# Loading and turning the weights of a two-layer kernel ahead of its first transposes, and handing out the first slots after two tiles

## The chip, the cores and the metric

One core of a Trainium2 chip runs the whole program. The metric is the device time of one execution in microseconds (us), the median of three runs. The engines are TensorE (PE), VectorE (DVE), ScalarE (ACT), GpSimd (POOL) and SyncE (SP, which here only issues DMAs). Waits between them are semaphore waits written into each engine's own list of instructions.

## The reference, cut to what matters

```python
xn = _layernorm(x)                        # x: 16 sequences of 256 tokens, 128 wide
s = _L0_attn_ref(xn, ...)                 # a complex linear recurrence over time
g = _silu(_L0_ffn_ref(xn, ...))           # 32 experts, top 4, plus a shared expert of width 256
x = x + s * g
xn = _layernorm(x)
s = _L1_attn_ref(xn, wq, bq, wk, bk, wv, bv)      # softmax attention
g = _silu(_L1_ffn_ref(xn, ...))           # 8 experts, top 2
x = x + s * g
```

In the first layer only the experts that a token chose are computed. So tokens must be routed: every token gets a row ("slot") in a list sorted by expert for each of its 4 choices.

## The kernel before, in words

The 4096 tokens are 32 tiles of 128. They are handled in two halves of 16 tiles (HT = 16, NH = 2), in groups of 4 tiles (GT = 4). For each half:

1. SP loads the rows of x (L403 to L405, all eight groups first, then the router's weights, then twelve loads of weights, L422, all counted on `w_in`). After them come two copies of `expert_sel`, six fills of `slot_rows0` with zeros (L434), the experts' weights and six fills of `slot_rows1`.
2. DVE normalises the rows (`norm0`, L1183 to L1206). PE transposes each group (`turn_half`, L608), ACT copies the result out of PSUM (`copy_half`, L956), PE multiplies it with the router's weights (L580), ACT copies the logits (L945).
3. DVE finds the four highest logits of each tile (`route`, L1224 to L1233), group by group, and writes `picked`, ones where an expert was chosen. PE counts (`ranks`, L593): bank 6 gets how many tokens of the same tile stand before each token, bank 7 the totals of each tile. From them DVE works out the slots: it copies bank 7 to SBUF turned to expert-major (L1239), makes a running sum over the tiles (L1240), the first tile of each expert (L1244 to L1250), adds that to all sums (L1251), adds bank 6 (L1253), and then picks out the four slots of every token in two pieces, first 4 tiles and then 12 (L1258 to L1270). Each piece raises `slots_ready`. After the first piece it also hands `tile_ex` to PE, which returns the expert of every slot tile.
4. POOL waits for the zero fills of the half (`filled`) and for `slots_ready`, and sends every tile's rows to their slots with indirect DMAs (L549), 4 for each tile, 64 for each half. Before tile 4 it waits for the second piece.

In the first half PE does the second layer's weights after the ranks (L620 to L635: a product of wq and wk, a transpose of wv, four columns with biases, eight transposes and some small products, into banks 2 to 5), and ACT copies them to SBUF after `exp_top` (L968 to L972). Then the shared expert of the first half runs (`shared_in`, `shared_out`, L648 to L661; ACT's silu L979, DVE's product L1309 and its gated result L1314), while POOL sends. In the second half, norm, transposes and logits follow, then the route of the second half with the shared expert's steps set between its links (`beside`), and three more recurrences (L1337 to L1345). Then 48 stages of expert work follow, 24 for each half (PE L718, L743, L726, L734; ACT L1000, L1006, L1024, L1015; DVE L1404), which read the slots that POOL wrote, and the gathers of their results (POOL L563), and at last the second layer.

SP starts loading the slots of a half when all 64 sends of that half have landed (`sent`).

The order of all this is written out by hand. Every engine runs its own list in order, and a wait holds all that is behind it on that engine.

Of the kernel before, what the change touches and what calls it, by code (L numbers as in the profile page):

```python
# [22 lines left out]
P = 128  # L23
# [22 lines left out]
EPS = 1e-5  # L46
SCALE = float(P) ** -0.5
# [79 lines left out]
def build(nc, x, phazor, phazor_init, last_re, last_im, router_w, w_gate, w_up, w_down, sh_gate, sh_up,  # L127
# [10 lines left out]
    with ctx:  # L138
# [69 lines left out]
        tot_em = route_tmp[:, 0, :].rearrange("p (e t) -> p e t", e=E0)  # L208
# [77 lines left out]
        zero_set = sem("zero_set")  # L286
        filled = [sem(f"filled{r}") for r in range(NH)]
# [109 lines left out]
        def _(sp):  # L397
# [4 lines left out]
            for g in range(NG):  # L402
                sp.dma_start(x_tok[:, g * GT:(g + 1) * GT, :],  # L403
                             x_rows[:, g * GT:(g + 1) * GT, :]).then_inc(x_in[g], 16)
# [19 lines left out]
            assert n == N_W  # L424

# [58 lines left out]
        def _(pool):  # L484
# [57 lines left out]
            for r in range(NH):  # L542
                pool.wait_ge(filled[r], 16 * N_FILL)
                for t in range(HT):
                    if t in (0, GT):
                        pool.wait_ge(slots_ready, r * 2 + 1 + t // GT)
# [22 lines left out]
        def _(pe):  # L569
# [14 lines left out]
            def ranks(r):  # L584
# [3 lines left out]
                for g in range(HT // GT):  # L588
                    pe.wait_ge(picked_ready, r * HT // GT + g + 1)
                    of = picked[:, g * GT * TOP0:(g + 1) * GT * TOP0, :].rearrange("p (t k) e -> p t k e", k=TOP0)  # L590
                    for to, rows_before in ((6, not_before), (7, ones_bf)):
                        for k in range(TOP0):
                            mm = pe.matmul(ps[:, to, g * w:(g + 1) * w], rows_before[:], of[:, :, k, :],  # L593
                                           start=(k == 0), stop=(k == TOP0 - 1))
# [19 lines left out]
            turn_half(0)  # L614
            ranks(0)

            pe.wait_ge(w_in, 16 * N_W)
            pe.wait_ge(lg_sb, NG // NH)

            pe.matmul(ps[:, 2, 0:P], raw1[:, 0, :], raw1[:, 1, :], start=True, stop=True)  # L620
            pe.transpose(ps[:, 2, P:2 * P], raw1[:, 2, :], ident[:])
            pe.matmul(ps[:, 2, 2 * P:2 * P + 1], raw1[:, 0, :], bqk[:, 1:2], start=True, stop=True)
            pe.matmul(ps[:, 2, 2 * P + 1:2 * P + 2], raw1[:, 1, :], bqk[:, 0:1], start=True,
                      stop=True).then_inc(wT_ps, 1)
            for j in range(CH1):
                last = pe.transpose(ps[:, 3, j * P:(j + 1) * P], raw_fc[:, j, :], ident[:])
# [11 lines left out]


            tile_ids(0)  # L640
            pe.wait_ge(wT_sb, 4)
# [288 lines left out]
        def _(sc):  # L930
# [34 lines left out]
            copy_half(0)  # L965
            exp_top(0)
            sc.wait_ge(wT_ps, 4)
            a.copy(w1T[:], bank(2, 2 * P + 2)).then_inc(wT_sb, 1)  # L968
            a.copy(fcT[:].rearrange("p a b -> p (a b)"), bank(3)).then_inc(wT_sb, 1)
            a.copy(prT[:].rearrange("p a b -> p (a b)"), bank(4)).then_inc(wT_sb, 1)  # L970
            a.copy(g1T[:], bank(5, E1))
            a.copy(bv_all, ps[0:3, 5, P:P + VW]).then_inc(wT_sb, 1)  # L972

# [200 lines left out]
        def _(dve):  # L1174
# [3 lines left out]
            v.memset(zeros[:, 0:GW], 0.0).then_inc(zero_set, 1)  # L1178

# [32 lines left out]
            def route(r, beside=None):  # L1212
# [7 lines left out]
                for g in range(HT // GT):  # L1220
# [8 lines left out]
                    if g == HT // GT - 1:  # L1229
# [9 lines left out]
                link(v.tensor_copy(tot_em, bank(7).rearrange("p (t e) -> p e t", t=HT)))  # L1239
                link(v.tensor_tensor_scan(cum_em.rearrange("p e t -> p (e t)"), not_first.rearrange("p e t -> p (e t)"),  # L1240
                                          tot_em.rearrange("p e t -> p (e t)"), 0.0, ALU.mult, ALU.add))
# [9 lines left out]
                link(v.tensor_tensor(cum_em, cum_em,  # L1251
                                     tiles_e[:].rearrange("p (e a) -> p e a", a=1).to_broadcast([P, E0, HT]), ALU.add))
                link(v.tensor_tensor(pos, bank(6).rearrange("p (t e) -> p t e", t=HT),  # L1253
                                     cum_em.rearrange("p e t -> p t e"), ALU.add))

                for c, (a, b) in enumerate(((0, GT), (GT, HT))):
# [39 lines left out]
            v.memset(ones_bf[:], 1.0)  # L1296
            v.memset(ones[:], 1.0)
            link(v.memset(not_first, 1.0))
            link(v.memset(not_first[:, :, 0:1], 0.0))
# [324 lines left out]
```

## Time and profile before

| what | us |
|---|---|
| median of three runs (711.32 to 712.45) | 712.23 |
| the profiled execution, whole | 712.29 |
| its span in the trace | 710.5 |
| busy: PE | 404.0 (57%) |
| busy: DVE | 324.1 (46%) |
| busy: POOL | 269.1 (38%) |
| busy: ACT | 259.3 (36%) |

No engine is busy all the time, so the shares alone name no bound. The page must be read by stage: its second part, 40 slices of 17.8 us with a digit for each engine's busy share, has POOL at 7 for slices 4 to 6 and 10 to 14 while the other engines fall to 0 in some of the same slices. What stands in those stretches has to be read in the timeline, engine by engine.

### The profile page before, as it was taken

How to read it: one execution, taken by the hardware profiler on the slowest of the kernel's cores; microseconds unless marked ns; L12 is line 12 of the kernel's file. 1: busy time of each engine (PE TensorE's matmuls, PEld its weight loads, DVE VectorE, ACT ScalarE, POOL GpSimd, SP SyncE). 2: the span in 40 equal slices, each digit the busy share in tenths (PEclk: the TensorE clock that was granted, in tenths of full speed). 3: DMA queues.
4: the chain of work that ended last, by engine and by line, in shares of the span. 5: the costliest groups of instructions: out<-in, count | busy, mean ns of one | idle time of the engine just before them, and what ended most of it. 6: DMA issues, size and time to landing. Idle time of an engine off the chain costs nothing. (4 is left out here: it accounts for less than half of the span.)

```text
span 710.5 us, 8856 instructions
## 1 busy us (share of the span) xinstructions
PE 404.0 (57%) x2582; PEld 364.4 (51%) x2582; DVE 324.1 (46%) x1167; ACT 259.3 (36%) x505; POOL 269.1 (38%) x324
## 2 busy tenths in 40 slices
PE   0873020676332019999512929299721674897996
PEld 0752020565321019999512919298610563786885
DVE  7871200486740015765000415068600491988853
ACT  1410000241000006767201515166411372886985
POOL 7467775001777730000474262500577166000000
PEclk9977555688655559999865968689955697998999
DMA  7999212000112114552521524242211011000000
GB/s 187 362 278 403 71 52 74 30 0 9 48 63 68 52 44 134 168 170 95 168 62 52 175 78 134 74 134 90 64 52 53 19 54 51 16 16 15 10 23 24
DMA packets 45903, 65.17 MB, mean 92 GB/s; under 512 B 8586, under 2 KB 23331, under 8 KB 45859
## 3 DMA queue, kind: packets, MB, share of 16 engines
q1 hardware_dynamic: 37666, 47.83, 21.1%
q0 software_dynamic: 8192, 16.79, 7.8%
q8 instruction: 23, 0.38, 0.2%
q14 instruction: 22, 0.17, 0.1%
HBM read 28.93 MB, written 35.65 MB: 91 GB/s over the span
## 5 line engine op out<-in xcount | busy, mean ns | idle before, releaser
L549 POOL DMA_INDIRECT slot_rows<-xn_tok,slot_of x128 | 125.6, 981 | 104.9 <-DVE slot_of L1270 66.4
L563 POOL DMA_INDIRECT onehot<-expert_rows,slot_of x64 | 61.8, 966 | 185.0 <-DMA expert_rows<-zeros 131.5
L1404 DVE TENSOR_TENSOR act<-sg,ps 128x384 f32<-128x384 f32 x48 | 26.6, 554 | 161.2 <-issue 101.0
L563 POOL DMA_INDIRECT route_tmp<-expert_rows,slot_of x64 | 60.7, 948 | 36.2 <-issue 19.0
L743 PE MATMUL ps<-w_gu,raw_fc 128*128 x192 | 41.0, 363 | 41.8 <-ACT raw_fc L1000 38.7
L734 PE MATMUL ps<-w_dn,actT 96*128 x384 | 54.0, 286 | 18.3 <-issue 15.9
L1006 ACT ACTIVATE sg<-ps 128x384 f32<-128x384 f32 x48 | 23.5, 491 | 106.8 <-remote 67.7
L661 PE MATMUL ps<-shd,hs_h 128*128 128x128 f32 x128 | 21.5, 321 | 70.1 <-issue 40.1
L734 PEld LDWEIGHTS ps<-w_dn,actT 96*128 96x128 f32 x384 | 49.2, 201 | 19.7 <-issue 19.6
L743 PE MATMUL ps<-w_gu,raw_pr 128*128 x192 | 40.2, 358 | 31.9 <-issue 31.7
L661 PEld LDWEIGHTS ps<-shd,hs_h 128*128 128x128 f32 x128 | 19.7, 228 | 73.8 <-issue 41.3
L743 PEld LDWEIGHTS ps<-w_gu,raw_fc 128*128 128x128 f32 x192 | 35.3, 214 | 43.1 <-issue 42.9
L979 ACT ACTIVATE hs_t<-ps 128x512 f32<-128x512 f32 x16 | 9.4, 597 | 118.3 <-remote 81.7
L743 PEld LDWEIGHTS ps<-w_gu,raw_pr 128*128 128x128 f32 x192 | 34.8, 211 | 32.9 <-issue 32.9
L1565 DVE TENSOR_TENSOR rows<-rows,ps 128x1024 f32<-128x1024 f32 x16 | 19.5, 1219 | 70.3 <-PE ps L886 45.0
L820 PE MATMUL ps<-prT,rows 128*128 128x128 f32 x256 | 36.4, 293 | 16.4 <-issue 10.8
L820 PEld LDWEIGHTS ps<-prT,rows 128*128 128x128 f32 x256 | 32.7, 203 | 19.5 <-issue 19.3
L726 PE MATMUL ps<-ident,act 128*96 128x128 f32 x192 | 31.1, 288 | 19.5 <-issue 19.5
L1015 ACT COPY zeros<-ps 128x512 f32<-128x512 f32 x48 | 28.1, 586 | 28.2 <-PE ps L734 16.0
L718 PE MATMUL ps<-ident,rows 128*128 128x128 f32 x192 | 33.1, 301 | 5.5 <-DMA rows<-slot_rows 3.9
L726 PEld LDWEIGHTS ps<-ident,act 128*96 128x96 f32 x192 | 23.0, 134 | 21.1 <-issue 20.5
L1024 ACT COPY actT<-ps 96x512 f32<-96x512 f32 x48 | 28.0, 584 | 11.3 <-remote 10.6
(242 smaller groups left out, 919.2 us busy)
## 6 DMA issues: line engine op xcount, KB each, us to landing
slot_rows<-zeros SPq DMA_DIRECT2D x12, 1024.0 KB, 9.7
rows<-slot_rows SPq DMA_DIRECT2D x48, 256.0 KB
expert_rows<-zeros SPq DMA_DIRECT2D x48, 256.0 KB, 2.0
x_tok<-in_L_attn_x_dram SPq DMA_DIRECT2D x8, 256.0 KB, 4.9
slot_rows<-xn_tok,slot_of POOLq DMA_INDIRECT x128
out_dram<-raw_fc SPq DMA_DIRECT2D x16, 128.0 KB
w_dn<-in_L_ffn_w_down_dram SPq DMA_DIRECT2D x1, 1536.0 KB
onehot<-expert_rows,slot_of POOLq DMA_INDIRECT x64
```

The costliest lines, as they stand in the source:

```text
L549: g.indirect_dma_start(out=slot_rows[r], out_offset=bass.IndirectOffsetOnAxis(ap=slot_of[:, n:n + 1], axis=0), in_=xn_tok[:, r * HT + t, : ...
L563: g.indirect_dma_start(out=gath[b % 4][:, j, :], out_offset=None, in_=expert_rows[r], in_offset=bass.IndirectOffsetOnAxis(ap=slot_of[:, n: ...
L661: mm = pe.matmul(ps[:, 4 + u, j * P:(j + 1) * P], hs_h[u][:, c, j * P:(j + 1) * P], shd[:, c, :], start=(c == 0), stop=(c == 1))
L718: mm = pe.transpose(ps[:, 0, j * P:(j + 1) * P], rows[slot][:, j * P:(j + 1) * P], ident[:])
L726: mm = pe.transpose(ps[0:I0, 5, j * P:(j + 1) * P], act[u][:, j, :], ident[:])
L734: mm = pe.matmul(ps[:, 6, j * P:(j + 1) * P], actT[u][:, j * P:(j + 1) * P], w_dn[:, bass.ds(e[j] * P, P)], start=True, stop=True)
L743: mm = pe.matmul(ps[:, 1 + 2 * u + j // 2, (j % 2) * 256:(j % 2) * 256 + 2 * I0], exT[u][:, j * P:(j + 1) * P], w_gu[:, bass.ds(e[j], 1), ...
L820: mm = pe.matmul(ps[:, 3, j * P:(j + 1) * P], hg[u][:, c, j * P:(j + 1) * P], prT[:, c, :], start=(c == 0), stop=(c == CH1 - 1))
L1006: a.activation(sg[u][:].rearrange("p (a b) i -> p a b i", a=2), ps[:, 1 + 2 * u:3 + 2 * u, :].rearrange("p a (b i) -> p a b i", b=2)[:, :, ...
L1015: a.copy(eo[slot], bank(6)).then_inc(e_out, 1)
L1024: a.copy(actT[u][:], ps[0:I0, 5, :]).then_inc(e_aTs, 1)
L1404: v.tensor_tensor(act[u][:].rearrange("p (a b) i -> p a b i", a=2), sg[u][:].rearrange("p (a b) i -> p a b i", a=2), ps[:, 1 + 2 * u:3 + 2 ...
```

## The change

- SP loads x's rows of the first half, then the router's weights, then the twelve loads of weights, and x's rows of the second half last.
- DVE clears `ones_bf`, `ones` and `not_first` at the start and not after `norm0(0)`.
- PE waits for all twelve loads and turns the weights before the first half's transposes, into banks 6, 7, 4 and 5. ACT copies them before it copies the first transposes. PE's ranks wait for those copies.
- PE writes the totals into bank 7 expert-major, so that DVE's copy L1239 goes and the running sum reads PSUM.
- The two pieces of slots are of 2 and 14 tiles (`FIRST = 2`), and the additions L1251 and L1253 are made for each piece. POOL waits for the second piece before tile 2.

```diff
+FIRST = 2
 ...
-            for g in range(NG):
-                sp.dma_start(x_tok[:, g * GT:(g + 1) * GT, :],
-                             x_rows[:, g * GT:(g + 1) * GT, :]).then_inc(x_in[g], 16)
+            def load_x(r):
+                for g in range(r * NG // NH, (r + 1) * NG // NH):
+                    sp.dma_start(x_tok[:, g * GT:(g + 1) * GT, :],
+                                 x_rows[:, g * GT:(g + 1) * GT, :]).then_inc(x_in[g], 16)
+
+            load_x(0)
             sp.dma_start(rw[:, 0:E0], router_w).then_inc(rw_in, 16)
...
             assert n == N_W
+            load_x(1)
...
-                    if t in (0, GT):
-                        pool.wait_ge(slots_ready, r * 2 + 1 + t // GT)
+                    if t in (0, FIRST):
+                        pool.wait_ge(slots_ready, r * 2 + 1 + t // FIRST)
...
-                            mm = pe.matmul(ps[:, to, g * w:(g + 1) * w], rows_before[:], of[:, :, k, :],
-                                           start=(k == 0), stop=(k == TOP0 - 1))
+                            if to == 6:
+                                into, chosen = ps[:, 6, g * w:(g + 1) * w], of[:, :, k, :]
+                            else:
+
+                                into = bank(7).rearrange("p (e t) -> p e t", t=HT)[:, :, g * GT:(g + 1) * GT]
+                                chosen = of[:, :, k, :].rearrange("p t e -> p e t")
+                            mm = pe.matmul(into, rows_before[:], chosen, start=(k == 0), stop=(k == TOP0 - 1))
...
-            turn_half(0)
-            ranks(0)
-
             pe.wait_ge(w_in, 16 * N_W)
-            pe.wait_ge(lg_sb, NG // NH)
+            pe.wait_ge(ones_set, 1)
+
+            pe.matmul(ps[:, 6, 0:P], raw1[:, 0, :], raw1[:, 1, :], start=True, stop=True)
...
+            turn_half(0)
+            pe.wait_ge(wT_sb, 4)
+            ranks(0)
 
             tile_ids(0)
-            pe.wait_ge(wT_sb, 4)
...
-            copy_half(0)
-            exp_top(0)
             sc.wait_ge(wT_ps, 4)
-            a.copy(w1T[:], bank(2, 2 * P + 2)).then_inc(wT_sb, 1)
+            a.copy(w1T[:], bank(6, 2 * P + 2)).then_inc(wT_sb, 1)
...
+            copy_half(0)
+            exp_top(0)
...
             v.memset(zeros[:, 0:GW], 0.0).then_inc(zero_set, 1)
+            v.memset(ones_bf[:], 1.0)
+            v.memset(ones[:], 1.0).then_inc(ones_set, 1)
+            link(v.memset(not_first, 1.0))
+            link(v.memset(not_first[:, :, 0:1], 0.0))
...
-                link(v.tensor_copy(tot_em, bank(7).rearrange("p (t e) -> p e t", t=HT)))
                 link(v.tensor_tensor_scan(cum_em.rearrange("p e t -> p (e t)"), not_first.rearrange("p e t -> p (e t)"),
-                                          tot_em.rearrange("p e t -> p (e t)"), 0.0, ALU.mult, ALU.add))
+                                          bank(7), 0.0, ALU.mult, ALU.add))
...
-                link(v.tensor_tensor(cum_em, cum_em,
-                                     tiles_e[:].rearrange("p (e a) -> p e a", a=1).to_broadcast([P, E0, HT]), ALU.add))
-                link(v.tensor_tensor(pos, bank(6).rearrange("p (t e) -> p t e", t=HT),
-                                     cum_em.rearrange("p e t -> p t e"), ALU.add))
-
-                for c, (a, b) in enumerate(((0, GT), (GT, HT))):
+                for c, (a, b) in enumerate(((0, FIRST), (FIRST, HT))):
+                    link(v.tensor_tensor(cum_em[:, :, a:b], cum_em[:, :, a:b], tiles_e[:]
+                                         .rearrange("p (e a) -> p e a", a=1).to_broadcast([P, E0, b - a]), ALU.add))
+                    link(v.tensor_tensor(pos[:, a:b, :], ps[:, 6, a * E0:b * E0].rearrange("p (t e) -> p t e", e=E0),
+                                         cum_em[:, :, a:b].rearrange("p e t -> p t e"), ALU.add))
```

## Rows read from the trace of the kernel before

**Rows 1.** The page's head.

```profile
span 710.5 us, 8856 instructions
```

**Rows 2.** Timeline, first half's sends: start, duration, instruction [idle before, releaser].

```profile
38.80 1.23 POOL L549 DMA_INDIRECT slot_rows<-xn_tok,slot_of  x1 [12.09 <-DVE slot_of L1270]
...
97.22 0.60 ACT L979 ACTIVATE hs_t<-ps 128x512 f32<-128x512 f32 x1 [33.73 <-remote]
...
119.33 0.97 POOL L549 DMA_INDIRECT slot_rows<-xn_tok,slot_of  x1 [0.31 <-issue]
...
128.75 1.08 ACT L979 ACTIVATE hs_t<-ps 128x512 f32<-128x512 f32 x2 [30.93 <-remote]
```

**Rows 3.** Timeline, the second half's sends.

```profile
174.66 0.97 POOL L549 DMA_INDIRECT slot_rows<-xn_tok,slot_of  x1 [54.36 <-DVE slot_of L1270]
...
204.93 0.37 ACT L982 COPY xnT<-ps 128x256 f32<-128x256 f32 x1 [3.26 <-PE ps L670]
...
214.78 0.58 ACT L1000 COPY raw_pr<-ps 128x512 f32<-128x512 f32 x1 [8.33 <-remote]
...
256.21 0.97 POOL L549 DMA_INDIRECT slot_rows<-xn_tok,slot_of  x1 [0.30 <-issue]
...
263.77 0.58 ACT L1000 COPY raw_fc<-ps 128x512 f32<-128x512 f32 x1 [6.51 <-remote]
```

**Rows 4.** Timeline, DVE, the first half's route from the ranks on.

```profile
30.01 0.69 DVE L1239 COPY route_tmp<-ps 128x512 f32<-128x512 f32 x1 [1.08 <-PE ps L593]
...
33.35 0.69 DVE L1251 TENSOR_TENSOR route_tmp<-route_tmp,tiles_e 128x512 f32<-128x512 f32 x1
34.08 1.00 DVE L1253 TENSOR_TENSOR route_tmp<-ps,route_tmp 128x512 f32<-128x512 f32 x1
35.11 0.90 DVE L1258 TENSOR_TENSOR onehot<-picked,route_tmp 128x128 f32<-128x128 bf16 x4
36.05 0.69 DVE L1262 TENSOR_REDUCE top_f<-onehot 128x16 f32<-128x512 f32 x1
...
37.68 0.17 DVE L1270 CUSTOM_DVE_ANT_0 slot_of<-slot_of,slot_a 128x32 uint16<-128x32 uint16 x1
...
40.98 1.75 DVE L1262 TENSOR_REDUCE top_f<-onehot 128x48 f32<-128x1536 f32 x1
...
43.92 0.21 DVE L1270 CUSTOM_DVE_ANT_0 slot_of<-slot_of,slot_a 128x96 uint16<-128x96 uint16 x1
```

**Rows 5.** Timeline, DVE, the ends of the two pieces in the second half.

```profile
173.71 0.17 DVE L1270 CUSTOM_DVE_ANT_0 slot_of<-slot_of,slot_a 128x32 uint16<-128x32 uint16 x1
...
187.78 0.21 DVE L1270 CUSTOM_DVE_ANT_0 slot_of<-slot_of,slot_a 128x96 uint16<-128x96 uint16 x1
```

**Rows 6.** Timeline, loads, first transposes and the weights; the transposes of the second half.

```profile
14.38 0.51 SPq L422 DMA_DIRECT2D raw_pr<-in_L_ffn_w_proj_dram  x1
...
16.00 2.04 PE L608 MATMUL ps<-ident,xn_tok 128*128 128x128 f32 x8 [16.00 <-DVE xn_tok L1206]
...
17.12 0.58 ACT L956 COPY xnT<-ps 128x512 f32<-128x512 f32 x1 [7.81 <-PE ps L608]
...
29.81 0.44 PE L620 MATMUL ps<-raw 128*128 128x128 f32 x2
...
32.25 0.37 ACT L968 COPY w1T<-ps 128x258 f32<-128x258 f32 x1 [2.54 <-PE ps L635]
...
33.53 0.25 ACT L972 COPY mth<-ps 3x129 f32<-3x129 f32 x1
...
141.48 0.63 PE L608 MATMUL ps<-ident,xn_tok 128*128 128x128 f32 x4
```

**Rows 7.** Timeline, DVE, first and last of the four groups' top-4 search.

```profile
20.12 0.47 DVE L1224 MAX8 top<-logits 128x8 f32<-128x32 f32 x4
...
28.25 0.69 DVE L1233 TENSOR_TENSOR picked<-iota_e,top_i 128x512 bf16<-128x512 f32 x1
```

**Rows 8.** Silus L1006 alone in one window: ACT busy (count), granted clock, DMA.

```profile
270.00:334.00 64.00, 9.80 (x20) 1.00 0.48 152
```

More of the change, by code:

```diff
@@ L207, in build @@
         route_tmp = sb("route_tmp", [P, 4, HT * E0])
-        tot_em = route_tmp[:, 0, :].rearrange("p (e t) -> p e t", e=E0)
         cum_em = route_tmp[:, 1, :].rearrange("p (e t) -> p e t", e=E0)
@@ L286, in build @@
         zero_set = sem("zero_set")
+        ones_set = sem("ones_set")
         filled = [sem(f"filled{r}") for r in range(NH)]
@@ L612, in turn_half @@
                 logits_of((r + 1) * NG // NH - 1)
-            turn_half(0)
-            ranks(0)
             pe.wait_ge(w_in, 16 * N_W)
-            pe.wait_ge(lg_sb, NG // NH)
[L620 to L623, printed above, removed]
+            pe.wait_ge(ones_set, 1)
+            pe.matmul(ps[:, 6, 0:P], raw1[:, 0, :], raw1[:, 1, :], start=True, stop=True)
+            pe.transpose(ps[:, 6, P:2 * P], raw1[:, 2, :], ident[:])
+            pe.matmul(ps[:, 6, 2 * P:2 * P + 1], raw1[:, 0, :], bqk[:, 1:2], start=True, stop=True)
+            pe.matmul(ps[:, 6, 2 * P + 1:2 * P + 2], raw1[:, 1, :], bqk[:, 0:1], start=True,
                       stop=True).then_inc(wT_ps, 1)
             for j in range(CH1):
-                last = pe.transpose(ps[:, 3, j * P:(j + 1) * P], raw_fc[:, j, :], ident[:])
+                last = pe.transpose(ps[:, 7, j * P:(j + 1) * P], raw_fc[:, j, :], ident[:])
             last.then_inc(wT_ps, 1)
@@ L963, in copy_half @@
                              ACT.Sigmoid).then_inc(sh_gated, 1)
-            copy_half(0)
-            exp_top(0)
             sc.wait_ge(wT_ps, 4)
-            a.copy(w1T[:], bank(2, 2 * P + 2)).then_inc(wT_sb, 1)
-            a.copy(fcT[:].rearrange("p a b -> p (a b)"), bank(3)).then_inc(wT_sb, 1)
+            a.copy(w1T[:], bank(6, 2 * P + 2)).then_inc(wT_sb, 1)
+            a.copy(fcT[:].rearrange("p a b -> p (a b)"), bank(7)).then_inc(wT_sb, 1)
             a.copy(prT[:].rearrange("p a b -> p (a b)"), bank(4)).then_inc(wT_sb, 1)
@@ L1295, in _ @@
             norm0(0)
[L1296 to L1299, printed above, removed]
             dve.wait_ge(pool_c, 7)
```

## The prediction

> **What bounds the kernel now.** I read the page's slices first, then the timeline of POOL, then that of ACT in the same stretches. The span is 710.5 us [rows 1]; the profiled execution took 712.29 us, 0.06 above the median of the runs, so a sum made against it stands for the median too. The reader is to see two bursts. POOL's 64 sends of the first half start at 38.80 and the last starts at 119.33 [rows 2], a step of 80.53 / 63 = 1.28 us each. Those of the second half run from 174.66 to 256.21 [rows 3]. Nothing in the trace makes a send shorter than this. The first send of each burst is released by DVE's slot numbers, L1270 [rows 2, 3]; neither the zero fills nor the ids came last. Inside the bursts ACT, and with it PE and DVE, comes to a near stop for a reason that the profile gives only as "remote": an idle of 33.73 us before one silu [rows 2], 8.33 us before one copy [rows 3], while the producer had long finished. They run again shortly after the burst: ACT takes up at 128.75, which is 8.4 us after the last send's end (119.33 + 0.97), and at 263.77, which is 6.6 us after 256.21 + 0.97 [rows 2, 3]. Between the bursts (128.75 to 174.66) the work is a chain through DVE and PE that ends in the second half's slots. So the end of the program is, to first order: start of burst one + burst one + the chain + burst two + a tail. An edit is worth what it does to the starts and lengths of the bursts.
>
> **Edits with one answer.** The early clears (four DVE instructions, under 1 us in all) go into the time in which DVE waits for its first data; at the old place they delayed nothing that was last, since the first logits came later. I cost them at nothing. If that cover were gone they would cost that 1 us. The second half's rows are loaded last, some 8 us later than before, but DVE reads them only after the first route ends at 44.13 [rows 4], so nothing waits. SP's list has the same number of loads ahead of the zero fills, so the fills start as before, and POOL's first wait had ended before 38.80.
>
> **Shorter chain to the first slots (in both halves).** Two slopes come from rows. L1262 takes 0.69 us for 512 elements and 1.75 for 1536 [rows 4], so 1.04 ns for an element and 0.16 fixed. L1258 takes 0.90 for four of 128 [rows 4], and I give it the same slope. Then:
> - L1239 goes: 0.69 us and a link's gap of 0.04, as between L1251 and L1253 [rows 4]: 0.73.
> - L1251 for 2 tiles, 64 elements, by that law 0.23 against 0.69: 0.46 less.
> - L1253 for 64 elements: between 1.00 / 8 and its full 1.00; its fixed part and its own slope give about 0.26, so 0.74 less.
> - L1258 at 64 elements: 4 x 64 x 1.04 ns = 0.27 less. L1262 at 256: 0.27 less.
> Sum 2.47 us less. Against it stands the scan, which now reads PSUM. No row has that. The nearest is L1253, 1.00 with a PSUM operand against L1251's 0.69 for the same 512 elements [rows 4]; so 0 to +0.31. I take 0, since L1253 also turns its order, and the plain copy L1239 out of PSUM costs 0.69, as much as L1251 in SBUF. The Trainium skill (VectorE: DVE Perf Modes, "Why PSUM operands drop a tier") says that a PSUM operand only costs the faster modes, and fp32 with two tensors has none of them. By that rule the scan costs 0 more; the rows of L1253 allow the 0.31, and the sum would be 2.2 instead of 2.47. PE's totals are read and written with a stride now: 16 small matmuls in a half, for which no row gives a price. Below by 0 (the old order), above by each taking twice as long, which adds about 0.4 for the last group; I take 0.
>
> **The second piece grows, and POOL waits for it sooner.** The second piece gets L1251 and L1253 for 14 tiles (448 elements: 0.62 + 0.88 + two gaps of 0.04), 4 x 64 more elements in L1258 (0.27) and 256 more in L1262 (0.27): 2.1 us. POOL has 8 sends now and not 16 before it needs that piece.
> - First half: the pieces ended at 37.85 and 44.13 [rows 4], 6.28 apart; now 8.4. POOL's first send came 0.95 after the first piece, its ninth could go 0.95 + 8 x 1.28 = 11.2 after it. The piece plus the 0.95 is 9.3. No wait, 1.9 us to spare.
> - Second half: there the shared expert's steps stand between the pieces, which ended at 173.88 and 187.99 [rows 5], 14.1 apart; now 16.2. The ninth send could go 0.8 + 8 x 1.28 = 11.0 after the first piece, but must wait until 16.2 + 0.8 = 17.0. That is a pause of 6.0 us. Before, the seventeenth was due at 0.8 + 16 x 1.28 = 21.3 with its slots there at 14.9, so there was none. Behind POOL's wait are 56 sends, and behind those SP's loads and all gathers.
> Net effect on the end of burst two, counted from the ranks of the second half: 6.0 - 2.47 = +3.5 us.
>
> **Weights ahead of the first half.** The last of the weights was issued at 14.38 + 0.51 = 14.89 [rows 6]. With four loads of x behind it instead of ahead it is issued some 3.3 us earlier, and I estimate that it lands at 14.5 (bounds 13.5 and 17). PE would start with the transposes of rows at 16.00 [rows 6]; now it first does the weights. Those took from 29.81 to 32.25 [rows 6], 2.4 us, but at PE's fast pace. At 16.00 PE is at its slow one: eight transposes in 2.04 us against four in 0.63 at 141.48 [rows 6]. So 4.4 us rather than 2.4: 14.5 to 18.9. ACT's copies took 32.25 to 33.78, 1.5 us, plus 0.2 to start [rows 6]: 20.6. Only then ACT copies the first transposes, before at 17.12 [rows 6]. That is 3.5 us late, on the path to the slots. What it frees was hidden: PE and ACT stood idle behind the ranks.
> What follows depends on PE's pace. If it stays slow as before, the route is 3.5 us late. If eight dense transposes and the weights bring the fast pace earlier, the first logits come 0.9 earlier, DVE's four searches, 20.12 to 28.94 [rows 7], of which about 0.7 were waits, run closed up, and the ranks take half of their 1.07 (28.94 to 30.01 [rows 4, 7]), 0.5 less: 3.5 - 2.1 = 1.4 late. With the 2.47 from above the first send moves by +1.0 or by -1.1. I take the middle, 0, since the trace has cases of either pace and none with this order.
>
> **Sum.** 712.29 + 0 (burst one) + 3.5 (burst two) = 715.8 us, 3.5 over the profiled execution and as much over the median. With the bounds of the terms (-1.1 to +1.0, the scan 2 x 0.3, the stride 2 x 0.4, the landing up to 2.5 more, not all at once) the forecast's own range is 714.3 to 719.
>
> **Rivals.**
> - *The pause feeds the stalled engines: faster.* ACT's lateness builds up within a burst: at 204.93, 30 us after 174.66, it still follows PE at once, and before 214.78 it idles for 8.33 [rows 3]. A pause of 6 us in POOL at about 182 to 188 may reset what runs down, so that ACT, PE and DVE do two or three expert stages more before the burst's end. In the clear stretch behind, 20 silus L1006 stand in 64 us [rows 8], a stage of 3.2 us, so 715.8 - 2.5 x 3.2 = 707.8, or 704 with four. It decides from the second stage on (715.8 - 6.4 = 709.4, below the time before). For it: lateness grows with time in a burst, and no pause lies inside either. Against: the burst goes on for 71 us after the pause, and in burst one ACT had stood idle since 97.22 - 33.73 = 63.5, 25 us into the burst [rows 2]. The Trainium skill (Runtime: NRT & Kernel Launch, "Instruction fetch mechanics") says that each sequencer fetches its instructions over a DMA queue of its own, ahead of use; by that a pause would let the fetches catch up, as this rival wants, though the same section calls the cost mostly hidden, and no row here shows a fetch.
> - *The end of burst two does not set the tail: no change.* Then POOL's later end is hidden, and what counts is DVE's chain to the end of the second piece: -2.47 + 2.1 = -0.4, so 712.29 - 0.4 and the first half's -1.1 to +1.0: 711.9. For it: no instruction of the first 24 stages needs the second half's sends. Against: in both bursts ACT takes up only after the last send [rows 2, 3].
> - *The stop comes earlier: clearly slower.* The new part of burst two starts near 188, and burst one stopped ACT sooner than burst two did. Then the turned recurrences (3.26 + 0.37 = 3.6 us each at 204.93 [rows 3]) and the first expert stages fall into the stop and are done after the burst: three recurrences at 3.6 us or one to three stages at 3.2, so 4 to 10 us more: 720 to 726. It decides when ACT is late by a copy of the recurrences.
> - *The first burst gains:* w_in lands early and PE's fast pace comes at once, and POOL's pause is shorter than reckoned since the shared steps shrink: 710.
>
> **How the numbers follow.** Forecast 0.45 (714.3 to 719); the feeding pause 0.22 (704 to 710.5); tail not set by burst two 0.15 (711 to 713.6); earlier stop 0.13 (720 to 726); first burst gains 0.05 (708 to 710.5). Within 0.2% (1.4 us, about what a measurement of this kernel can tell from no change) is 710.8 to 713.7: 0.16, nearly all of it the third. Faster: 0.26, from the second and the last. Slower: 0.58. The range that leaves 2 in 10 out cuts both far ends: 707 to 721.
>
> **What would show it.** The row L1239 is gone, and L1251 and L1253 appear twice in a half, with 64 and 448 elements. The weights' copies L968 to L972 come ahead of the first L956, which starts at 20 to 21. The first send stands within 1.2 us of 38.80. In the second half POOL has a wait of 6 us on DVE's `slot_of` after eight sends: that is the step on which the forecast rests. ACT takes up 6 to 9 us after the last send. The forecast is wrong if that pause is absent, if ACT has done more than two silus (L1006) when the burst ends, or if it takes up well before the last send.

## The result and the profile after

| | before | after |
|---|---|---|
| median of five runs, us | 712.17 (711.32 to 712.45) | 715.67 (715.18 to 716.65) |
| the profiled execution, us | 712.29 | 715.18 |
| its span, us | 710.5 | 713.4 |

The changed kernel takes 1.0053 times as long, with a 95% interval of 1.0036 to 1.0069. It is slower by 3.5 us, and 715.8 was forecast. That the sum met the time was luck: two of its terms were wrong in size, its central step was wrong in kind, and the errors cancelled. The views of after show most of that.

The page's head, and the timeline of POOL in after (start, duration, instruction, idle before and who ended it): burst one's first send, burst two's first, eighth, ninth and last:

```profile
span 713.4 us, 8859 instructions
```

```profile
41.11 1.22 POOL L554 DMA_INDIRECT slot_rows<-xn_tok,slot_of  x1 [14.51 <-DVE slot_of L1280]
...
177.19 0.96 POOL L554 DMA_INDIRECT slot_rows<-xn_tok,slot_of  x1 [54.59 <-DVE slot_of L1280]
...
186.53 0.97 POOL L554 DMA_INDIRECT slot_rows<-xn_tok,slot_of  x1 [0.30 <-issue]
190.98 0.96 POOL L554 DMA_INDIRECT slot_rows<-xn_tok,slot_of  x1 [3.48 <-DVE slot_of L1280]
...
262.64 0.96 POOL L554 DMA_INDIRECT slot_rows<-xn_tok,slot_of  x1 [0.30 <-issue]
```

Against [rows 2, 3]: burst one starts 2.31 us later (38.80 to 41.11), burst two 2.53 later (174.66 to 177.19), and its last send starts 6.43 later (256.21 to 262.64). The pause is there, after eight sends, but 3.48 us long and not 6.0. The later start and the pause make 5.7 of the 6.43; the rest is sends that take longer than 0.97 us, of which after has a little more than before.

The timelines of PE and ACT in after where the weights are turned, which answer to [rows 6]:

```profile
14.77 0.77 PE L627 MATMUL ps<-raw 128*128 128x128 f32 x2 [14.77 <-DMA raw_pr<-in_L_ffn_w_proj_dram]
```

```profile
19.08 0.38 ACT L974 COPY w1T<-ps 128x258 f32<-128x258 f32 x1 [9.76 <-PE ps L642]
...
20.51 1.05 ACT L964 COPY xnT<-ps 128x512 f32<-128x512 f32 x2
```

The weights have landed at 14.77 and are turned by 19.04. The first copy of transposes starts at 20.51 against 17.12.

The timeline of DVE in after, the first half's route, which answers to [rows 4]:

```profile
34.83 1.22 DVE L1251 TENSOR_TENSOR_SCAN route_tmp<-route_tmp,ps 128x512 f32<-128x512 f32 x1 [2.52 <-PE ps L604]
...
37.43 0.23 DVE L1263 TENSOR_TENSOR route_tmp<-route_tmp,tiles_e 128x64 f32<-128x64 f32 x1
37.69 0.26 DVE L1265 TENSOR_TENSOR route_tmp<-ps,route_tmp 128x64 f32<-128x64 f32 x1
37.98 0.63 DVE L1268 TENSOR_TENSOR onehot<-picked,route_tmp 128x64 f32<-128x64 bf16 x4
38.65 0.42 DVE L1272 TENSOR_REDUCE top_f<-onehot 128x8 f32<-128x256 f32 x1
...
39.99 0.17 DVE L1280 CUSTOM_DVE_ANT_0 slot_of<-slot_of,slot_a 128x16 uint16<-128x16 uint16 x1
```

The chain from its first link to the end of the first piece is 34.83 to 40.16, 5.33 us. Before it was 30.01 to 37.85, 7.84 [rows 4]. That is 2.51 less. But DVE now waits 2.52 us for PE's ranks and not 1.08.

The timeline of PE, the last counts of a half (`not_before` into bank 6, `ones_bf` the totals into bank 7). The first fence is after, the second before:

```profile
33.33 0.60 PE L604 MATMUL ps<-picked,not_before 128*128 128x128 bf16 x4
33.73 1.06 PE L604 MATMUL ps<-picked,ones_bf 128*128 128x128 bf16 x4
...
166.75 0.40 PE L604 MATMUL ps<-picked,not_before 128*128 128x128 bf16 x4
166.99 1.03 PE L604 MATMUL ps<-picked,ones_bf 128*128 128x128 bf16 x4
```

```profile
160.40 0.39 PE L593 MATMUL ps<-picked,not_before 128*128 128x128 bf16 x4
...
161.96 0.39 PE L593 MATMUL ps<-picked,ones_bf 128*128 128x128 bf16 x4
```

In after, the totals' operand is read with a stride and the result is written in runs of four; four of them take 1.03 us in the second half, where the same work in order took 0.39. The ranks there last from 163.48 to 168.02, 4.5 us, against 160.40 to 162.35, 1.95.

The timeline of DVE in after, the second half's route: the scan, a step of the shared expert, and the ends of the two pieces, which answer to [rows 5]:

```profile
168.06 1.22 DVE L1251 TENSOR_TENSOR_SCAN route_tmp<-route_tmp,ps 128x512 f32<-128x512 f32 x1 [0.81 <-PE ps L604]
...
170.48 0.69 DVE L1315 TENSOR_TENSOR hs_h<-hs_t,ps 128x512 f32<-128x512 f32 x1 [1.19 <-ACT hs_t L987]
...
176.25 0.17 DVE L1280 CUSTOM_DVE_ANT_0 slot_of<-slot_of,slot_a 128x16 uint16<-128x16 uint16 x1
...
190.49 0.22 DVE L1280 CUSTOM_DVE_ANT_0 slot_of<-slot_of,slot_a 128x112 uint16<-128x112 uint16 x1
```

The 2.5 us that the chain saves are given back in waits for PE (0.81) and for ACT (1.19), which itself follows PE, and by a later start.

Last, the timeline of ACT in burst two, its silus L1014 (L1006 before). The first fence is after, the second before:

```profile
210.69 0.49 ACT L1014 ACTIVATE sg<-ps 128x384 f32<-128x384 f32 x1 [1.94 <-issue]
212.52 0.49 ACT L1014 ACTIVATE sg<-ps 128x384 f32<-128x384 f32 x1 [1.34 <-PE ps L751]
...
229.46 0.49 ACT L1014 ACTIVATE sg<-ps 128x384 f32<-128x384 f32 x1 [10.68 <-remote]
...
268.66 0.58 ACT L1023 COPY zeros<-ps 128x512 f32<-128x512 f32 x1 [17.61 <-remote]
270.15 0.49 ACT L1014 ACTIVATE sg<-ps 128x384 f32<-128x384 f32 x1 [0.91 <-remote]
```

```profile
234.36 0.49 ACT L1006 ACTIVATE sg<-ps 128x384 f32<-128x384 f32 x1 [19.00 <-remote]
256.76 0.49 ACT L1006 ACTIVATE sg<-ps 128x384 f32<-128x384 f32 x1 [21.91 <-remote]
```

The busy time by windows (window, length, then PE, PE's weight loads, DVE, ACT and POOL with counts, granted clock, DMA share, GB/s), first after, then before:

```profile
200.00:264.00 64.00, 18.25 (x78) 15.61 (x78) 9.36 (x16) 5.72 (x11) 48.67 (x50) 0.61 0.21 67
```

```profile
200.00:264.00 64.00, 10.84 (x36) 8.49 (x36) 7.57 (x12) 3.13 (x7) 43.77 (x45) 0.53 0.17 56
```

With the pause in burst two, PE issues 78 matmuls in the same 64 us and not 36, and three silus have begun when the burst ends, against two. So although the burst ends 6.4 us later, the fourth silu comes at 270.15 against 271.23, the 24th at 335.12 against 334.79, and the first gather starts at 344.52 against 343.86. In this pair the tail does not follow the end of the burst; how far one profile of a kernel stands from another is shown below.

### The profile page after: what moved, and what is told of

Read it like the earlier page. It is cut to its first block and busy times, and to the rows that moved or that the text cites. A ratio compares the mean times of both kernels' runs of the same rounds, so it can differ in the third digit from the quotient of the medians.

```text
span 713.4 us, 8859 instructions
## 1 busy us (share of the span) xinstructions
PE 417.6 (59%) x2582; PEld 375.5 (53%) x2582; DVE 322.4 (45%) x1169; ACT 259.0 (36%) x505; POOL 269.3 (38%) x324
## 5 line engine op out<-in xcount | busy, mean ns | idle before, releaser
L742 PE MATMUL ps<-w_dn,actT 96*128 x384 | 55.8, 292 | 35.1 <-ACT zeros L1023 19.2
L742 PEld LDWEIGHTS ps<-w_dn,actT 96*128 96x128 f32 x384 | 50.2, 204 | 37.1 <-issue 37.1
L1014 ACT ACTIVATE sg<-ps 128x384 f32<-128x384 f32 x48 | 23.5, 490 | 76.4 <-PE ps L751 36.0
L877 PE MATMUL ps<-xn_tok,fcT 128*128 128x256 f32 x128 | 33.8, 412 | 0.0
```

The costliest lines, as they stand in the source:

```text
L742: mm = pe.matmul(ps[:, 6, j * P:(j + 1) * P], actT[u][:, j * P:(j + 1) * P], w_dn[:, bass.ds(e[j] * P, P)], start=True, stop=True)
L877: mm = pe.matmul(ps[:, 4 + c // 2, (c % 2) * SEQ:(c % 2 + 1) * SEQ], fcT[:, c, :], turned_rows(b), start=True, stop=True)
```

## The experiments

Ratios are against the kernel before on the same chip, with a 95% interval. Burst two is given from its first send's start to its last send's end: 174.66 to 257.18 before, 177.19 to 263.60 after. "Theory A" is the forecast's mechanism: the starts and ends of the bursts set the time. "B" is its rival: a pause feeds the stalled engines. None of these kernels leaves out anything of the computation.

### Undoing parts of the change

**Weights back behind the first half's ranks.** Edit of after:

```diff
+            turn_half(0)
+            pe.wait_ge(ones_set, 1)
+            ranks(0)
...
-            turn_half(0)
+            tile_ids(0)
             pe.wait_ge(wT_sb, 4)
-            ranks(0)
-
-            tile_ids(0)
```

ACT's copies of the weights go back behind `exp_top(0)`, and the banks are 2 and 3 again.

> The changed kernel with the weights' work put back behind the first half's ranks (banks 2 to 5, ACT's copies after exp_top); load order, early clears, turned totals and pieces of 2 and 14 tiles stay. Theory A (the burst's end sets the tail, and the weights are what delays burst one): first send at 37.7 to 38.0 (changed kernel: 41.11), everything behind it 3.1 to 3.4 earlier, whole time 712.3. Rival B (the delay of burst one comes from the totals' strided matmuls, the weights are hidden): first send at 40 or later, time 714.5 or more.

Measured: 0.9975 [0.9943, 1.0008]. The first send starts at 37.74 against 41.11 in after, 3.37 earlier, which is what the placement costs. Burst two runs from 174.38 to 261.21 with its pause (184.60 to 188.30). Rival B of the expectation, that the weights are hidden, falls: it asked for a first send at 40 or later.

**The totals read in order, written with a stride.** Edit of after:

```diff
-    into = bank(7).rearrange("p (e t) -> p e t", t=HT)[:, :, g * GT:(g + 1) * GT]
-    chosen = of[:, :, k, :].rearrange("p t e -> p e t")
+    into = bank(7).rearrange("p (e t) -> p t e", t=HT)[:, g * GT:(g + 1) * GT, :]
+    chosen = of[:, :, k, :]
```

> The changed kernel, with the totals' matmuls reading picked in its own order and writing bank 7 with a stride instead (same result in bank 7). If the strided read is what makes L604 take 1.06 us for four instead of 0.60: 0.60 again, the first half's ranks end 1.4 to 1.7 us earlier, first send at 39.5 to 39.7, the second half's scan no longer waits for PE; time 713 to 714. If the strided write costs as much: L604 stays at 1.06 and the time at 715.7.

Measured: 0.9986 [0.9955, 1.0017]. The timeline of PE in this kernel, four totals of the first half and the last counts of the second:

```profile
30.00 1.06 PE L604 MATMUL ps<-picked,ones_bf 128*128 128x128 bf16 x4
...
162.13 0.43 PE L604 MATMUL ps<-picked,not_before 128*128 128x128 bf16 x4
162.40 0.60 PE L604 MATMUL ps<-picked,ones_bf 128*128 128x128 bf16 x4
```

In the second half four totals take 0.60 us with the stride in PSUM, 1.03 with that in the operand, and 0.39 with none. The ranks there last 2.8 us and not 4.5, and DVE's scan no longer waits for them. In the first half, at PE's slow pace, the stride in PSUM takes 1.06, as much as the other; only the third and fourth group of totals, from 32.56 on, take less (0.75 and 0.60). So the first send gains less than was expected: it is at 40.30, 0.81 earlier than in after and not 1.4 to 1.6. Burst two runs from 172.17 to 258.99.

**The first piece of four tiles again.** Edit of after:

```diff
-FIRST = 2
+FIRST = 4
```

> The changed kernel with FIRST = 4 (pieces of 4 and 12 tiles): no pause in burst two. First send 1.0 later than 41.11, the second half's first piece 1.0 later too. Theory A (only the end of burst two counts): burst two ends 2 to 3 us earlier than 263.60, time 713.5. Rival B (the pause lets ACT, PE and DVE run on, which bought the changed kernel nearly two expert stages): burst two ends earlier, but ACT has only two silus of expert work done by its end, and the time is 717 to 720.

Measured: 1.0029 [1.0003, 1.0054]. Burst two runs from 179.32 to 261.88 without a pause. That starts 2.1 us later than in after and ends 1.7 earlier. By A the time should be 1.7 us less than that of after, a ratio of 1.0029, and that is what was measured; B had asked for 717 to 720 us where before takes 712.2, a ratio of 1.007 or more. In the profile, though, the 24th silu comes at 339.62 (335.12 in after) and the first gather at 348.69 (344.52). The timeline of ACT in this kernel, the only silus before the end of the burst:

```profile
238.58 0.49 ACT L1014 ACTIVATE sg<-ps 128x384 f32<-128x384 f32 x1 [19.71 <-remote]
...
260.98 0.49 ACT L1014 ACTIVATE sg<-ps 128x384 f32<-128x384 f32 x1 [21.91 <-remote]
```

They are two again, as late as in before, as B says. The profiled execution was 4 us above this kernel's median, so the 4.5 us at the silu are not read as a size. This kernel does not decide between A and B: its time fits A, its silus fit B.

**Both: weights at the old place and totals read in order.** The edits of the first two together.

> Both edits: weights at their old place and the totals read contiguously. Both theories: first send at 36.3 to 36.6, which is 2.3 earlier than before the change (38.80). Theory A with a pause of 3 us in burst two: time 709.5 to 711. If stalls inside the bursts swallow or add more than that: anything from 707 to 714.

Measured: 0.9935 [0.9905, 0.9966], so the rest of the change alone gains. The first send is at 37.41, 1.4 earlier than in before and not 2.3, since the stride in PSUM costs PE 1.06 us for four in this kernel's first half too. Burst two runs from 166.94 to 253.89, the 24th silu is at 326.29. Between the bursts lie 47.8 us and not 54.4 [rows 2, 3], much more than the chain gives; in the first experiment it is 55.2, in the second 50.2. Which part of that is the edit and which the way the stop ended is not shown. From the pairs on this chip the weights' place costs 0.9986 - 0.9935 = 0.5% (3.6 us), and the strided operand 0.9975 - 0.9935 = 0.4% (2.9 us). Each ratio has some 0.3% of its own on either side, so the sizes are rough. Put on top of 0.9935 they give 1.0026 and not the 1.0053 of the whole change, which was measured on another chip; whether they add up is not shown.

**The weights' place alone.** The kernel before with the new order of loads, weights first, and early clears, everything else as before. The core of the edit:

```diff
-            turn_half(0)
-            ranks(0)
-
...
-            pe.wait_ge(lg_sb, NG // NH)
+            pe.wait_ge(ones_set, 1)
...
+            turn_half(0)
+            pe.wait_ge(wT_sb, 4)
+            ranks(0)
```

> The kernel before with only the weights' part of the change (load order, early clears, weights turned and copied ahead of the first transposes); route, totals and pieces of 4 and 12 tiles as before. Reckoned in the prediction: first copy of transposes 3.5 us late, and the route with it. Theory A: first send at 41.9 to 42.3 (before 38.8), burst two ends 3.1 to 3.4 later, time +3.3, ratio 1.0045. Rival (PE's fast pace comes sooner and gives it back): first send at 40.2, ratio 1.002.

Measured: 1.0055 [1.0019, 1.0091]. The first send is at 42.24, 3.4 us later than in before, and burst two runs from 178.47 to 260.87. This part alone costs as much as the whole change. A later start of the bursts does carry through to the end here, about as A says; what follows asks whether a gap inside a burst does.

### What the end of burst two does to the tail

**The kernel before once more**, for how far one profile stands from another.

> The kernel before, unchanged, for its trace on the chip of these runs. Every theory: bursts as in its first trace within 1 us, two silus of expert work (L1006) done when burst two ends, the 24th some 77.6 us behind that end.

Measured: 710.0. Bursts 38.85 to 120.37 and 173.47 to 256.67, two silus in burst two (218.54, 240.23), and the 24th at 330.86, 74.2 after the burst's end; in the first profile of before it was 77.6 after it. So differences of some 3 us in the stall are within what one profile can vary, and single differences below that are not read here. The last stretch varies as much: from the end of the last gather to the end of the span it is 112.3 us here and 109.6 in the first profile of before.

**Only the pause.** The kernel before, in which POOL waits for the second piece before tile 2, though its slots are of four tiles:

```diff
-                    if t in (0, GT):
-                        pool.wait_ge(slots_ready, r * 2 + 1 + t // GT)
+                    if t in (0, 2):
+                        pool.wait_ge(slots_ready, r * 2 + 1 + t // 2)
```

> The kernel before, where POOL alone waits for the second piece of slots ahead of tile 2 and not of tile 4; nothing else. In burst one that wait is over in time; in burst two it makes a gap of about 3 us after 8 sends (173.88 to 187.99, less 11). Theory A (a later end of burst two is a later end): 712.2 + 3 = 715 to 716, ratio 1.004. Rival B (the gap lets ACT run on): three silus done at the end of burst two instead of two, the 24th silu 70 to 72 us behind that end instead of 77.6, ratio 0.994 to 0.997.

Measured: 0.9978 [0.9955, 1.0002]. The timeline of POOL in this kernel, its ninth send:

```profile
187.69 0.96 POOL L549 DMA_INDIRECT slot_rows<-xn_tok,slot_of  x1 [3.45 <-DVE slot_of L1270]
```

Burst two ends at 260.31, 3.6 us later than in the second profile of before and 3.1 later than in the first, and the time is not longer; by A it had to be 3 to 4 us longer, 1.004 to 1.005, which the interval leaves out. Three silus have begun before the end (207.14, 209.24, 224.72), and the 24th comes 71.3 us after it, as B says. A falls here: the pause on which the forecast's loss rested costs nothing.

**A pause in the middle.** The kernel before with six memsets of POOL, linked by waits, after 32 of the 64 sends of burst two:

```diff
+                    if r == 1 and t == HT // 2:
+                        for _ in range(6):
+                            chain.link(g.memset(idle[:], 0.0))
```

> The kernel before, with six linked POOL memsets of 128x512 bf16 (some 3.5 us) in burst two ahead of tile 8, that is after 32 sends; nothing else. Theory A: +3.5 us, ratio 1.005. Rival B, any gap serves: ACT takes up in the gap, one or two stages more are done, ratio 0.995 to 1.000. Rival C, only an early gap serves (before ACT has come to its stop): as A.

Measured: 0.9898 [0.9847, 0.9949], so some 7 us gained (the medians give 5.8) by 3.7 us of delay. That is more than B expected, and C, by which only an early gap serves, falls. The timelines of POOL and of ACT in this kernel around the pause:

```profile
214.13 0.96 POOL L553 DMA_INDIRECT slot_rows<-xn_tok,slot_of  x1 [0.30 <-issue]
215.09 3.45 POOL L550 MEMSET idle<- 128x512 bf16 x6
218.82 0.97 POOL L553 DMA_INDIRECT slot_rows<-xn_tok,slot_of  x1 [0.28 <-POOL idle L550]
```

```profile
217.72 0.49 ACT L1010 ACTIVATE sg<-ps 128x384 f32<-128x384 f32 x1 [12.90 <-remote]
218.49 0.49 ACT L1010 ACTIVATE sg<-ps 128x384 f32<-128x384 f32 x1 [0.28 <-remote]
```

ACT had stood still for 12.90 us and takes up 2.6 us after the pause begins. Four silus have begun before the burst ends, and the 24th comes at 326.25.

**A pause after every eight sends of burst two.** The same edit with `if r == 1 and t and t % 2 == 0`.

> The kernel before, with such a pause of 3.5 us after every 8 sends of burst two (seven pauses, burst two 25 us longer); nothing else. Theory A: +25 us, ratio 1.034. Rival B: ACT runs in and behind each gap, some seven to fourteen stages of 3.2 us more are done inside the burst, ratio 0.97 to 1.00.

Measured: 0.9696 [0.9638, 0.9754]. Burst two runs from 173.76 to 282.58, its end 25.4 us later than in before [rows 3], and yet the kernel is 22 us faster: 17 silus have begun before it ends (the last at 282.39) and the 24th is at 306.89, 27.9 earlier.

### The stop in all trains of indirect DMAs

**Pauses everywhere, after every eight.** The kernel with both edits (0.9935 by itself) with six memsets after every eight sends in both bursts and after every eight gathers:

```diff
+                    if t and t % 2 == 0:
+                        for _ in range(6):
+                            chain.link(g.memset(idle[:], 0.0))
...
+                if b % (NSEQ // NH):
+                    for _ in range(6):
+                        chain.link(g.memset(idle[:], 0.0))
```

> The kernel of e4 (weights at their old place, contiguous totals, pieces of 2 and 14) with POOL pauses of 3.5 us (six linked memsets) after every 8 sends of both bursts, and after every 8 gathers. If a gap lets the stopped engines run wherever work waits: the gathers' bursts too shed stalls, ratio 0.94 to 0.96. Rival: burst one has only some 9 us of waiting work behind it and gets 25 us longer, so the ratio is 0.975 to 0.99, and worse than f3.

Measured: 0.8348 [0.8302, 0.8394]; 598.97 us. Both branches of the expectation had far less gain, 0.94 to 0.99.

**The same without the pauses of burst one.** Condition `if r == 1 and t > 2 and t % 2 == 0`.

> As f2, but no pauses in burst one (and none after the first 8 sends of burst two, where POOL waits for slots anyway). If only bursts with much other work waiting gain by pauses: ratio 0.94 to 0.96, 10 to 20 us better than f2. If the gathers are what the end waits for: no better than 0.97 - 0.0065, which is what e7 and e4 give together.

Measured: 0.8865 [0.8805, 0.8925]; 637.42 us. Both branches had this wrong too. So the pauses in burst one are worth 38 us (with the one after the first eight sends of burst two, which is gone as well, but there POOL waits for DVE's slots for 3.49 us). Yet burst one itself ends 25 us later with them, at 143.69 against 118.32. The timeline of POOL in the kernel with all pauses, the first send of burst two:

```profile
143.99 0.97 POOL L558 DMA_INDIRECT slot_rows<-xn_tok,slot_of  x1 [0.30 <-issue]
```

It follows burst one without a wait. Without the pauses it comes at 170.69, after 52.37 us of waiting for DVE: with them the norm, the ranks and the route of the second half run during burst one and not behind it. The gathers' pauses count as well: pauses in burst two alone (0.9696) and both edits (0.9935) would give 0.963 together, and with the gathers' it is 0.8865.

**Shorter pauses, after every four.** Three memsets after every four sends and every four gathers:

```diff
+                    if t:
+                        for _ in range(3):
+                            chain.link(g.memset(idle[:], 0.0))
...
+                    if j == TOP0:
+                        for _ in range(3):
+                            chain.link(g.memset(idle[:], 0.0))
```

> As f2, with the same total of pause cut finer: three linked memsets (some 1.75 us) after every 4 sends and every 4 gathers. If the share of free time is what counts: ratio 0.83, as f2. If a stop only builds up after some ten us of burst, so that shorter bursts never come to it: 0.80 or less. If a gap must have some length before the stopped engines take up: 0.86 or more.

Measured: 547.94 us against 712.3 for before, 0.7697 [0.7666, 0.7728]. It takes 23% less time than before, and after was slower than before. That is the second branch of the expectation (0.80 or less): cut finer, the same total of pauses gives more, so the share of free time is not all that counts. Its page, the head and POOL's share, and the digits of PE and ACT in 40 slices, and under that the same digits of after:

```profile
span 546.9 us, 9039 instructions
...
PE 393.9 (72%) x2582; PEld 358.1 (65%) x2582; DVE 328.6 (60%) x1169; ACT 256.4 (47%) x505; POOL 370.9 (68%) x504
...
PE   0877869551098999950878897948957799589995
...
ACT  1241144100045655630345554425784678568883
```

```profile
PE   1953202577442208999513929299811672997996
...
ACT  1500000142010005676201515266410662885985
```

The timeline of POOL in this kernel, a pause in burst one:

```profile
42.41 1.71 POOL L555 MEMSET idle<- 128x512 bf16 x3
44.39 0.98 POOL L558 DMA_INDIRECT slot_rows<-xn_tok,slot_of  x1 [0.28 <-POOL idle L555]
```

POOL is busier (68% against 38%), PE does the same 2582 matmuls, and of the five 0s in ACT's slices 3 to 7 of after, in the first burst, ACT has three left here, in slices 9 to 11 (each of 13.7 us and not 17.8). Added over all engines, the waits that the profile puts down to "remote" are 292.3 us in before, 252.3 with one pause in the middle, 149.3 with pauses after every eight everywhere, and 22.6 here. Most of them are ACT's, the rest DVE's. Little of the gain is PE's own work: the same matmuls keep it busy for 393.9 us and not 404.0, at a mean granted clock of 0.880 and not 0.785.

## Why the prediction was right and wrong

**The shorter chain: right.** Forecast 2.47 us less, measured 2.51 in the first half. By term: L1263 0.23 (forecast 0.23), L1265 0.26 (0.26), L1268 0.63 for four (0.90 - 0.27), L1272 0.42 (0.42). The scan out of PSUM takes 1.22, as much as L1240 took from SBUF in the second half of before, so the 0 that was taken was right. By the rule of the Trainium skill (VectorE: DVE Perf Modes, "Why PSUM operands drop a tier") a PSUM operand costs only the faster modes, and fp32 with two tensors has none. The trace agrees for the scan. It does not settle L1253, which took 1.00 with a PSUM operand against L1251's 0.69 [rows 4] and also turns its order.

**Weights first: mechanism right, the value taken wrong.** The first copy comes 3.39 us later (forecast 3.5), and PE's work on the weights takes 4.27 us (14.77 to 19.04, forecast 4.4). PE kept its slow pace, the branch that gave +1.0 for the first send, and not the middle, 0, that was taken. In the whole stretch to the ranks nothing ran closed up: the first search moved from 20.12 to 23.46 and the last from 28.25 to 31.62, 3.4 each [rows 7]. The last experiment of the first group, with this part alone, gives the 3.4 again. Averaging two branches of which only one can happen was the mistake; the trace had the slow pace in that very stretch.

**The totals' stride: wrong by size, and it undid the gain.** It was taken at 0 with a bound of 0.4 for the last group. Measured, four totals take 1.03 to 1.06 us and not 0.63 (slow pace) or 0.39 (fast). The bound asked only for the last group after the last search. But four groups of four totals follow one another, each behind its four counts. From one group to the next PE needs 1.28 us in the first half of after and 0.85 with nothing strided (in the kernel with the weights' place alone), so in the first half PE falls behind DVE, and DVE's wait grows from 1.08 to 2.52: +1.44. So the first send: +3.4 weights, -2.5 chain, +1.4 stride, together +2.3, as measured, and outside the 1.2 us about 38.80 that the prediction had given. In the second half all counts run at once behind `picked`. It ends at 164.59 and DVE's first link starts at 168.06, 3.47 later; before it was 161.63 and 164.19, 2.56. Then the wait of 1.19 for ACT's silu opens, since PE's shared steps stand behind the ranks. Burst two therefore starts 2.53 late: `picked` 2.96 late (2.3 of it from burst one), 0.91 more for the ranks, and the chain to the first piece only 1.33 shorter (9.69 to 8.36) and not 2.47. Not all of it is priced: `picked` comes 0.65 later than burst one explains, within what one profile varies.

**The pause: there, but half as long.** Forecast 6.0 from pieces 16.2 us apart; they are 14.3 apart (176.42 to 190.71), and the added 2.1 us of DVE's work vanished. Of the 14.11 us between the pieces before, DVE worked 8.07 and waited 6.04, of which 4.51 was one wait for ACT's silu; after, it worked 9.83 and waited 4.46. So 1.76 us of added work went into 1.58 us of waits that shrank. The step counted the distance between two events as if DVE had been busy all of it. 3.48 us of idle against 0.30 between other sends is a pause of 3.2.

**The end of burst two sets the tail: false.** Here the forecast failed in kind, and by its own sign: it was to be wrong if ACT had done more than two silus when the burst ended, and there are three, the third at 229.46. The last send came 6.4 us later, 24 stages were done only 0.3 later, and the kernel with the pause alone was not slower. What holds of the step is that a later start carries through; what does not is that a gap inside the burst counts as a delay. The rival that the pause feeds the stalled engines, given 0.22, is the mechanism. It was priced with two to four stages (with four its sum is 703.0 and not 704); the pause is worth about one stage (3 silus against 2), and so it pays back 3.2 us of pause rather than more. The evidence against it had been that ACT stops 25 us into a burst while the burst goes on for 71 us after the pause. It did not ask what a gap does before the stop. And that ACT takes up only after the last send, held against the second rival, misread the rows: a silu runs at 97.22 in the middle of an unbroken train [rows 2], and two run at 234.36 and 256.76. A stop can end without a gap, after 33.73 us or 19.00; a gap ends it sooner and lets more than one instruction through.

**Why the time was still met.** Forecast: 0 + 3.5. What happened: +2.5 at the start of burst two and +3.2 for its pause, of which the gained stage takes back all but 0.3 at the 24th silu. At the first gather it is +0.66, and at the end of the last gather burst +0.61 (600.91 to 601.52). The other 2.3 us of the 2.9 between the two spans appear in and just behind that burst. The timeline of ACT there, first before, then after:

```profile
595.90 0.37 ACT L1127 COPY w_gu<-ps 128x258 f32<-128x258 f32 x1 [7.61 <-remote]
```

```profile
602.83 0.37 ACT L1135 COPY w_gu<-ps 128x258 f32<-128x258 f32 x1 [12.75 <-remote]
```

The same copy is let go within the burst in before and only behind it in after. But that is no work of the change: the second profile of before, the same program, has the long last stretch too (112.3 us from the last gather's end; 111.9 in after, 109.6 in the first profile of before). So one pair of profiles can't say in which stretch the 3.5 us of the medians lie. What is shown is that the weights' place and the strided totals cost time and the rest of the change gains some, and that the forecast, which left the first send where it was and put the pause at 6.0, met the sum by luck. (The bounds that it names give 714.7 as the lower end of its range and not 714.3; the measured time lies within both.)

**What stays open.** The runs show that a long unbroken train of indirect DMAs from POOL stops the other engines for long, and that gaps shorten or avoid it. A gap serves whether POOL waits in it (3.45 us, the pause alone) or clears memory. They don't show what it is that runs down. The section of the Trainium skill that the prediction named (Runtime: NRT & Kernel Launch, "Instruction fetch mechanics") would fit an engine that is kept from its next instructions, though it calls the cost mostly hidden. The prediction said that no row shows a fetch. The page of the profile does list two queues for instructions; in after:

```profile
q8 instruction: 23, 0.38, 0.2%
q14 instruction: 21, 0.17, 0.1%
```

The packed trace has the time of each of their packets. In burst one of before one begins at 52.91, and the next only at 138.05, in after at 56.01 and 134.43. ACT's stops of 33.73 us (63.50 to 97.22) and of 43.50 us (76.26 to 119.76) lie whole between them, and when they end no packet of these queues has come. So it was not the arrival of instructions that ended these stops, as far as the trace records every packet. Any other path that POOL's DMAs share with the engines would still fit. Kernels that separate these weren't run.

## What to carry to other kernels

Where many indirect DMAs follow one another on GpSimd and other engines wait for "remote" with their producers long done, break the train: here 2.0 us without a send after every four made the kernel 23% faster (some 0.7% of it from the other edits), though POOL worked longer. A distance between two events is not busy time; before work is added between them, count the idle in it. A stride that saves a copy on one engine may cost another engine more: price it for all instructions of the group, not for the last.

## What the runs showed of the hardware that was not expected

- A train of indirect DMAs, each 0.97 us on POOL with 0.30 between them, brings ACT to a stop of up to 43.50 us in after (33.73 in before [rows 2]; the row below, timeline of ACT). In these two stops no packet of the instruction queues arrives. In the kernel with a pause in the middle, a gap of 3.7 us released ACT 2.6 us after the gap began. Pauses of 3.7 us after every eight leave 149.3 us of "remote" waits, of 2 us after every four 22.6, from 292.3 without.
- Totals of 128 columns in bf16 whose moving operand is read with a stride took 1.03 to 1.06 us for four, at the fast and at the slow pace alike. Written to PSUM with a stride they took 0.60 at the fast pace and 1.06 at the slow, and in order 0.39 at the fast and 0.63 at the slow. The profile's granted clock doesn't tell the two paces apart there: in after it is 1.00 from 29.4 to 35.0, where four counts take 0.60, and from 163.4 to 168.0, where they take 0.39 to 0.41.
- VectorE's scan over 512 elements takes 1.22 us out of PSUM and out of SBUF.

```profile
119.76 0.60 ACT L987 ACTIVATE hs_t<-ps 128x512 f32<-128x512 f32 x1 [43.50 <-remote]
```
